# A mixture-of-experts layer on one Trainium2 core: per-row expert weights move from VectorE to GpSimd, and the last normalisation from VectorE to ScalarE, in place

## The reference

```
x   = x + layernorm(attention(layernorm(x)))          # 16 heads of 16, causal
h   = layernorm(x)
scores = softmax(h @ router_weight.T + router_bias)   # 8 experts
topk_w, topk_idx = top_k(scores, 2)
gu  = h @ gate_up_proj[e] + gate_up_bias[e]           # 256 -> 2 x 512
gate = min(gu[:512], 7);  up = clip(gu[512:], -7, 7)
act = (up + 1) * gate * sigmoid(1.702 * gate)
y_e = act @ down_proj[e] + down_bias[e]               # 512 -> 256
x   = x + layernorm(sum over the row's two experts of topk_w * y_e)
```

## Time and profile before

| | |
|---|---|
| median of 3 runs | 2218.0 us (2215.66 to 2218.64) |
| the profiled execution's own time | 2212.91 us |
| its span, first to last instruction | 2211.2 us |
| attention stage | to about 1327 us |
| expert stage | about 1335 to 2143 us |
| combine stage | 2143.6 us to the end |

### The profile page before, as it was taken

One profiled execution on the slowest core, in us unless ns is written; L12 is line 12 of the kernel. 1 busy time (PEld: TensorE's weight loads), 2 busy tenths in 40 slices (PEclk: granted clock), 3 DMA queues, 4 the chain that ended last, 5 costly groups with the idle time before them and its releaser, 6 DMA issues. The chain is left out here.

```text
span 2211.2 us, 51864 instructions
## 1 busy us (share of the span) xinstructions
PE 1984.6 (90%) x13630; PEld 1303.7 (59%) x13631; DVE 1691.3 (76%) x6010; ACT 1131.8 (51%) x2648; POOL 959.5 (43%) x1567
## 2 busy tenths in 40 slices
PE   5899999999999999999989736999999999999950
PEld 4444444444444444444333326999999999999950
DVE  2877788888888888888878245878878788787868
ACT  4377777777777777777767621222222222222210
POOL 5223344455465555564545641333333333333326
PEclk9899999999999999999999958999999999999985
DMA  6525464645464546353553326878788877877866
GB/s 205 174 96 168 147 195 154 193 151 190 127 190 135 180 133 190 124 179 122 184 175 100 120 84 209 243 237 244 236 241 241 234 245 235 243 237 237 244 191 237
DMA packets 259626, 412.93 MB, mean 187 GB/s; under 512 B 37136, under 2 KB 194960, under 8 KB 253200
## 3 DMA queue, kind: packets, MB, share of 16 engines
q1 hardware_dynamic: 219856, 366.67, 51.1%
q0 software_dynamic: 29824, 35.54, 7.6%
q10 hardware_dynamic: 9792, 8.93, 1.5%
HBM read 288.30 MB, written 122.14 MB: 186 GB/s over the span
## 5 line engine op out<-in xcount | busy, mean ns | idle before, releaser
L751 ACT ACTIVATE pw<-ps_e 128x512 f32<-128x512 f32 (+3 forms) x1536 | 687.5, 494 | 282.4 <-PE ps_e L907 268.0
L1300 PE MATMUL ps_g<-x_t,w_gu 128*128 128x128 f32 x4384 | 541.6, 277 | 18.6 <-ACT x_t L1231 11.6
L1300 PEld LDWEIGHTS ps_g<-x_t,w_gu 128*128 128x128 f32 x4384 | 517.8, 192 | 47.3 <-issue 40.7
L520 DVE CUSTOM_DVE_ANT_0 summed<-ps_s,c 128x128 bf16<-128x128 f32 (+3 forms) x1024 | 479.6, 481 | 60.8 <-PE ps_s L888 56.4
L888 PE MATMUL ps_s<-ks,qs 96*128 96x512 bf16 (+3 forms) x1536 | 488.8, 333 | 27.3 <-DVE rmax L520 7.7
L907 PE MATMUL ps_e<-qs,ks 98*128 98x512 bf16 (+3 forms) x1536 | 484.1, 329 | 4.4 <-ACT pw L751 3.5
L523 DVE TENSOR_REDUCE cmax<-ps_s 128x1 f32<-128x512 f32 x512 | 351.3, 686 | 143.4 <-PE ps_s L888 137.7
L888 PEld LDWEIGHTS ps_s<-ks,qs 96*128 96x128 bf16 x1536 | 151.9, 100 | 357.3 <-DVE cmax L520 92.7
L926 PE MATMUL ps_o<-pw,vs 128*32 128x512 f32 (+3 forms) x3072 | 329.1, 501 | 5.1 <-ACT ot L765 2.9
L1252 ACT ACTIVATE d_y<-biased,weight 128x256 f32<-128x256 f32 x136 | 69.1, 508 | 482.0 <-DVE biased L1211 482.0
L435 POOL TENSOR_SCALAR_AFFINE_SELECT pw<-pw 128x512 f32<-128x512 f32 x256 | 163.0, 637 | 302.3 <-ACT pw L751 302.1
(11 more groups left out here) (144 smaller groups left out, 2229.5 us busy)
## 6 DMA issues: line engine op xcount, KB each, us to landing
w_gu<-in_gate_up SPq DMA_DIRECT2D x138, 1024.0 KB
qs<-qk_parts SPq DMA_DIRECT2D x192, 128.0 KB, 2.8
ks<-qk_parts SPq DMA_DIRECT2D x192, 128.0 KB, 2.9
qk_parts<-space SPq DMA_DIRECT2D x120, 192.0 KB
d_xin<-xs SPq DMA_DIRECT2D x139, 130.5 KB
v_aug<-space SPq DMA_DIRECT2D x32, 512.0 KB, 4.6
vs<-v_aug SPq DMA_DIRECT2D x32, 512.0 KB
o_t<-ot SPq DMA_DIRECT2D x64, 256.0 KB
```

What stands on the lines that cost most here:

```text
L520: dve.tensor_tensor_reduce(summed[:, m % RJ, 0:w], ps_s[:, m % RS, 0:w], after[:, HALF - w:HALF], 1.0, LOWEST, ALU.add, ALU.max, dst).then ...
L751: act.activation(pw[:, n % RP, 0:w], ps_e[:, n % RE, 0:w], ACT.Exp, scale=SCALE).then_inc(e_done, 1)
L1300: last = pe.matmul(ps_g[:, u, half, m % KI], w_gu[:, u, k, m * P:(m + 1) * P], x_t[:, u, k], start=(k == 0), stop=(k == KT - 1))
```

## The change

- `destine` leaves DVE and goes to POOL, in five instructions for four: the expert number less the tile's (`other`), is that zero, times the weights, and the sum of the two; and the copy of the place. It runs for tiles 0 to 3 ahead of the first `prepare`, and then `destine(n+3)` stands ahead of `prepare(n)`, that is right behind the add of tile n-1. The waits of PE and ACT on `taken` are as before.
- Padding rows are no longer zero: they come from a new tile `nobody`, which holds the partition number in column 260. The larger-of is gone.
- ACT starts the `x1` load behind the sigmoid of the first tile of a round.
- Combine stage: all 16 steps have buffers of their own and all loads are started at once; the normalisation is four ACT instructions a step (scale and shift), in place; DVE works out the shift; POOL adds in place.

```
@@ clear_ends
-                engine.dma_start(xs[bass.ds(row, P), :], blank[:, 0:ROW]).then_inc(zeros_out, 16)
+                engine.dma_start(xs[bass.ds(row, P), :], nobody[:]).then_inc(zeros_out, 16)
@@ attention stage, gpsimd
+            pool.memset(nobody[:], 0.0).then_inc(blank_set, 1)
+            pool.wait_ge(blank_set, 2)
+            pool.tensor_tensor(nobody[:, D + 4:D + 5], consts["row"], consts["zero"], ALU.add).then_inc(blank_set, 1)
@@ expert stage, vector: destine is gone from hidden and from the start
-                destine(n + 2, i + 1, u)
@@ expert stage, scalar
-                    if pairs.start == 0:
-                        load_x1(act, i)
                     for u in range(2):
                         n = i * 2 + u
                         rows(n + 2, u)
                         sigmoid(n + 1, 1 - u)
+                        if pairs.start == 0 and u == 0:
+                            load_x1(act, i)
@@ expert stage, gpsimd
+            def destine(n, i, u):
+                pool.wait_ge(x_in[u], i * 16 + 16)
+                pool.tensor_tensor(other[:, u], xin[:, u, D + 2:D + 4], expert_f[:, bass.ds(n, 1)].broadcast_to([P, TOPK]), ALU.subtract).then_inc(apart, 1)
+                pool.tensor_copy(place[:, bass.ds(n, 1)], xin[:, u, D + 4:D + 5]).then_inc(taken, 1)
+                pool.wait_ge(apart, n + 1)
+                pool.sem_inc(apart_seen, 1)
+                pool.tensor_scalar(is_it[:, u], other[:, u], 0.0, None, ALU.is_equal).then_inc(is_ready, 1)
+                pool.wait_ge(is_ready, n + 1)
+                pool.tensor_tensor(part_of[:, u], is_it[:, u], xin[:, u, D:D + 2], ALU.mult).then_inc(part_ready, 1)
+                pool.wait_ge(part_ready, n + 1)
+                pool.tensor_tensor(weight[:, bass.ds(n, 1)], part_of[:, u, 0:1], part_of[:, u, 1:2], ALU.add).then_inc(taken, 1)
@@
             with pool.Fori(1, TILES // 2) as i:
                 for u in range(2):
                     n = i * 2 + u
+                    destine(n + 3, i + 1 + u, 1 - u)
                     prepare(n, u)
                     pool.wait_ge(y_out, n * 16)
                     pool.sem_inc(y_free, 1)
                     add(u)
@@ combine stage, scalar
+            def normalise(n):
+                act.wait_ge(shift_ready, n + 1)
+                for c in range(NB):
+                    last = act.activation(moe[:, n, c], moe[:, n, c], ACT.Identity, scale=rstd[:, n, c:c + 1], bias=shift[:, n, c:c + 1])
+                last.then_inc(normed_ready, 1)
@@ combine stage, vector
-                for c in range(NB):
-                    last = dve.tensor_scalar(normed[:, n % 2, c], moe[:, n % RA, c], mv[:, n % 2, c, 0:1],
-                                             rstd[:, n % 2, c:c + 1], ALU.subtract, ALU.mult)
+                dve.scalar_tensor_tensor(shift[:, n], mv[:, n, :, 0], -1.0, rstd[:, n], ALU.mult, ALU.mult).then_inc(shift_ready, 1)
```

More of the change, by code:

```diff
@@ L145, in attention_layer @@
         blank = sb("blank", [P, 1024])
+        nobody = sb("nobody", [P, ROW])
         c16_in = pw[:, 8:10].rearrange("p a b -> p (a b)")[:, 0:const16.shape[1]]
@@ L313, in _ @@
             sp.dma_start(bias_r[:], router_bias.rearrange("(a e) -> a e", a=1).broadcast_to([P, E])).then_inc(c_weights_in, 16)
-            sp.wait_ge(blank_set, 1)
+            sp.wait_ge(blank_set, 3)
             sp.dma_start(acc[0:P], blank[:, 0:D]).then_inc(acc_zero, 16)
             sp.dma_start(xs[DUMMY:DUMMY + SPARE * P].rearrange("(c p) d -> p c d", p=P),
-                         blank[:, 0:ROW].unsqueeze(1).broadcast_to([P, SPARE, ROW])).then_inc(acc_zero, 16)
+                         nobody[:].unsqueeze(1).broadcast_to([P, SPARE, ROW])).then_inc(acc_zero, 16)
             for g in SLOTS:
@@ L1112, in expert_stage @@
         w_gu = sb("w_gu", [P, 2, KT, 2 * I])
+        other = sb("d_other", [P, 2, TOPK])
         is_it = sb("is_it", [P, 2, TOPK])
@@ L1135, in expert_stage @@
                                     "act_ready", "y_ps", "y_biased", "y_ready"))
+        apart, apart_seen = sem("d_apart"), sem("d_apart_seen")
         y_out, one_more = sem("d_y_out"), sem("d_one_more")
@@ L1174, in expert_of, with hidden @@
                 return dve.value_load(table[0:1, 1, bass.ds(n, 1)], min_val=0, max_val=E - 1)
[L1176 to L1187, removed]
+            def hidden(n, u):
                 e = expert_of(n)
@@ L1214, in _ @@
             dve.tensor_scalar(b_gu[:, :, KI:2 * KI], b_gu[:, :, KI:2 * KI], 1.0, None, ALU.add).then_inc(one_more, 1)
-            for u in range(2):
-                destine(u, 0, u)
             dve.wait_ge(one_more, 1)
-            hidden(0, 0, 0)
+            hidden(0, 0)
             with dve.Fori(0, TILES // 2) as i:
-                for n, b, u in ((i * 2 + 1, i, 1), (i * 2 + 2, i + 1, 0)):
-                    hidden(n, b, u)
+                for n, u in ((i * 2 + 1, 1), (i * 2 + 2, 0)):
+                    hidden(n, u)
                     bias_rows(n - 1, 1 - u)
@@ L1270, in _ @@
             pool.sem_inc(carried, 1)
+            for n in range(4):
+                destine(n, n // 2, n % 2)
             prepare(0, 0)
             add(0)
+            destine(4, 2, 0)
             prepare(1, 1)
@@ L1342, in combine_stage @@
     STEPS = 2 * B
-    RA, RO = 6, 3
     with ExitStack() as ctx:
@@ L1349, in sem @@
             return ctx.enter_context(nc.semaphore(name))
[L1351 to L1357, removed]
+        moe = sb("moe", [P, STEPS, NB, D])
+        stats = sb("e_stats", [P, STEPS, NB, 6])
+        mv = sb("e_mv", [P, STEPS, NB, 2])
+        std = sb("e_std", [P, STEPS, NB])
+        rstd = sb("e_rstd", [P, STEPS, NB])
+        shift = sb("e_shift", [P, STEPS, NB])
         pad = sb("e_pad", [P, 1])
[L1359 to L1362, removed]
+        moe_in = [sem(f"e_moe_in{n}") for n in range(STEPS)]
+        out_done = sem("e_out")
+        stats_ready, mv_ready, std_ready, rstd_ready, shift_ready, normed_ready, added = (sem("e_" + n) for n in (
+            "stats_ready", "mv_ready", "std_ready", "rstd_ready", "shift_ready", "normed_ready", "added"))
         acc_v = acc[P:].rearrange("(p s c) d -> s p c d", p=P, s=STEPS)
@@ L1369, in _ @@
         def _(sp):
[L1370 to L1374, removed]
             for n in range(STEPS):
-                if n + RA < STEPS:
-                    sp.wait_ge(normed_ready, n + 1)
-                    load(n + RA)
+                sp.dma_start(moe[:, n], acc_v[n]).then_inc(moe_in[n], 16)
+            for n in range(STEPS):
                 sp.wait_ge(added, n + 1)
-                sp.dma_start(out_v[n], res[:, n % RO]).then_inc(out_done[n % RO], 16)
-            for u in range(RO):
-                sp.wait_ge(out_done[u], len(range(u, STEPS, RO)) * 16)
+                sp.dma_start(out_v[n], moe[:, n]).then_inc(out_done, 16)
+            sp.wait_ge(out_done, STEPS * 16)
         @block.gpsimd
@@ L1389, in _ @@
                 pool.wait_ge(normed_ready, n + 1)
-                if n >= RO:
-                    pool.wait_ge(out_done[n % RO], n // RO * 16)
-                pool.tensor_tensor(res[:, n % RO], normed[:, n % 2], x1[:, n * NB:(n + 1) * NB], ALU.add).then_inc(added, 1)
+                pool.tensor_tensor(moe[:, n], moe[:, n], x1[:, n * NB:(n + 1) * NB], ALU.add).then_inc(added, 1)
         @block.scalar
@@ L1397, in _, with root @@
             act.preload_act_table(ACT.Sqrt)
-            for n in range(STEPS):
+            def root(n):
                 act.wait_ge(mv_ready, n + 1)
-                act.activation(std[:, n % 2], mv[:, n % 2, :, 1], ACT.Sqrt, bias=EPS).then_inc(std_ready, 1)
+                act.activation(std[:, n], mv[:, n, :, 1], ACT.Sqrt, bias=EPS).then_inc(std_ready, 1)
+            def normalise(n):
[3 more added lines that the diff above has]
+                last.then_inc(normed_ready, 1)
+            root(0)
+            for n in range(1, STEPS):
+                root(n)
+                normalise(n - 1)
+            normalise(STEPS - 1)
         @block.vector
@@ L1404, in moments @@
             def moments(n):
-                dve.wait_ge(moe_in[n % RA], (n // RA + 1) * 16)
+                dve.wait_ge(moe_in[n], 16)
                 for c in range(NB):
-                    last = dve.bn_stats(stats[:, n % 2, c], moe[:, n % RA, c])
+                    last = dve.bn_stats(stats[:, n, c], moe[:, n, c])
                 last.then_inc(stats_ready, 1)
@@ L1412, in moments, with scales @@
                 for c in range(NB):
-                    last = dve.bn_aggr(mv[:, n % 2, c], stats[:, n % 2, c])
+                    last = dve.bn_aggr(mv[:, n, c], stats[:, n, c])
                 last.then_inc(mv_ready, 1)
-            def normalise(n):
+            def scales(n):
                 dve.wait_ge(std_ready, n + 1)
-                dve.reciprocal(rstd[:, n % 2], std[:, n % 2]).then_inc(rstd_ready, 1)
+                dve.reciprocal(rstd[:, n], std[:, n]).then_inc(rstd_ready, 1)
```

(11 more changed lines are left out.)

## The result

The changed kernel takes 2279.7 us (median of 4 runs, 2277.7 to 2281.1), the kernel before 2218.3 on the same chip: a ratio of 1.0279, with a 95% interval of 1.0261 to 1.0296. It is 61 us slower. The profiled execution took 2279.2 us, with a span of 2277.4.

The account below looks back on a forecast made before the run. The prediction took DVE to set the loop's pace at 5.78 us a tile. Loop +53.8, start +0.5 and combine stage -16.7 made +37.6 us on the median of 2218.0, say 2255 us, range 2178 to 2297.

Parts of the forecast that it names:

- DVE loses `destine` and stops being the pace: Expert loop: DVE's pace falls from 5.78 to 5.11 us a tile, under PE's floor of 5.52.
- The landing: Expert loop: an add not started early lands about 5.7 us after the weights' issue, when the load's burst is through.
- The locked loop: Expert loop: POOL and PE lock over two tiles, 12.36 us or 6.18 a tile, +53.8 us; chance 0.64.
- six terms: Two-tile loop: landing 5.7, next add 0.8, its issue 1.56, `destine` 1.2, to PE 0.1, to the weights' issue 3.0 us.
- Combine stage: After the loop: without DVE collisions POOL's add of 2.34 us becomes the step, -16.7 us.
- Small edits: Start of the kernel: `nobody` costs nothing, `destine` of the first tiles on POOL +0.5 us.
- fair turns: Rival, loop: add and weight packets interleave, landing 4.5 us or less, 5.58 a tile, total 2167 to 2175; chance 0.18.
- Half way: Rival, loop: landings of 5.0 us or `destine` of 0.7, 5.8 to 5.9 a tile, 2204 to 2218; chance 0.12.
- worse: Rival, loop: PE's idle lowers its clock, or `destine` is 1.8 us; over 6.5 a tile, over 2298; chance 0.06.

Follow-up runs that it names:

- wait_x1_old: The changed kernel with `destine` one tile further ahead, before POOL's wait for the add's landing, and the `x1` load back at the head of ACT's round: 2165.5 us.
- longer: The changed kernel with three more dependent small POOL instructions in `destine`: 2346.0 us, ratio 1.0578 to the kernel before.
- wait_longer: The changed kernel with `destine` one tile further ahead, before POOL's landing wait, plus three more dependent small instructions in it: 2171.1 us, ratio 0.9800.
- one_input: The changed kernel with DVE's two products reading their second input from a PSUM tile of ones instead of SBUF: 2266.1 us, ratio 1.0230.
- combine_only: The kernel before with only the new combine stage: 2200.3 us, ratio 0.9920.
- in_the_wait: The changed kernel with `destine` one tile further ahead, between the preparation of an add and POOL's wait for the landing: 2172.1 us, ratio 0.9795.

## Why the prediction was right

The forecast was 2255, the time is 2280. The mechanism held step by step; two terms of the loop, `destine` and the add's issue, were too small.

- *DVE loses `destine` and stops being the pace.* Right, though before the change it also waited for products in 43 tiles. Now it waits for products in nearly every tile, and once POOL is out of the way (`wait_x1_old`) the loop runs at 5.53, the 5.52 forecast as PE's floor.
- *The landing.* The forecast gave 5.7 us behind the weights' issue. Between 1375 and 2200 us the changed kernel has a median of 5.64 and a mean of 5.61. The 116 adds that start between 0.9 us ahead of the issue and 1.0 behind all land 5.4 to 5.95 behind it, and none of their packets moves before nine tenths of the burst's have; with half a load the mean is 4.37.
- *The locked loop.* Forecast 5.7 + 0.8 + 1.56 + 1.2 + 0.1 + 3.0 = 12.36. In the walk above: 5.57 + 0.75 + 1.62 + 1.41 + 0.06 + 3.06 = 12.47. The adds shown start 0.27 and 0.02 behind the weights' issue, where 0.3 was forecast; over the loop that was no constant: they start from 0.8 ahead to 0.9 behind in turn where tiles alternate, and only half lie within 0.5. The landing stays put all the same, so nothing hung on it. `longer` and `wait_longer` show that the loop spans two tiles and that it is a loop.
- *The mis-sized terms.* The mean tile is 6.37, not 6.18: the loop came to +79.6 us where +53.8 was forecast, and this is all of the miss. The means of the six terms over 130 loops of the changed kernel say where it lies: landing 5.61 (-0.09 against the forecast), next add 0.84 (+0.04), issue 1.69 (+0.13), `destine` 1.43 (+0.23), to PE 0.09 (-0.01), to the weights' issue 3.09 (+0.09): 12.75, 0.39 more in two tiles. `destine` and the add's issue were priced without DVE beside them, and a little low even so. In `one_input`, where nothing stretches them, they are 1.28 and 1.62, and the loop's mean is 12.55. So about half of the miss is the stretching (up to 2.20 for `destine` and 2.12 for an issue); the rest is small: 0.14 of the two terms themselves, 0.07 on the way to the weights' issue. The landing, forecast 0.09 too high, took a little off the miss.
- *Combine stage.* -16.7 forecast, -17.7 in the profile, -17 alone: right, by the row that decides it, POOL's 2.34 us add. ACT's four took 2.08 us.
- *Small edits.* +0.5 forecast ahead of the loop, +4.3 seen, within what `combine_only` shows of the start's own drift.

Of the rivals, *fair turns* falls: landings near the weights' issue are 5.6, not 4.5. The Trainium skill (DMA: Bandwidth & Descriptors, Queues, rings and completion order) has each DMA engine go round its queues a packet at a time; by that rule one would expect a 128 KB add not to wait for a megabyte beside it. The trace doesn't bear this out: 1 packet of the add beside 239 of the weights, and the other 143 behind them. Whether the add's packets were ready to go by then, no run shows, so the cause of their waiting is open. The rival's time, 2167 to 2175, is nonetheless what `in_the_wait` reached, by another way: there PE doesn't wait for the landing at all. *Half way* falls too (6.37, not 5.8 to 5.9). Of *worse*, both halves came true in small part: `destine` reached 1.8 and more in some tiles, and the clock fell behind two of PE's new idle stretches, for 3.4 us of the loop.

## What to carry to other kernels

Before work is moved to an engine with time to spare, look at what it will stand behind in that engine's order: here 1.3 us of work on an engine that idled over 3 us a tile made the loop 80 us longer where it stood behind an instruction that waits for a DMA to land, and 24 to 34 us shorter (5.60 and 5.53 a tile against 5.78) where it stood ahead of that wait. If what waits for the moved work also sets off the transfer that delays it, the two lock; add up the loop once round, divide by the tiles that it spans, and compare with the pace. And where a forecast is taken from quiet rows, ask which instructions of the neighbour engine will lie beside it.

## What the hardware showed

- A POOL instruction of 128 x 2 elements (`is_it`) takes 0.21 us, and 0.57 to 0.67 while DVE runs a product with two inputs in SBUF; the issue of an indirect DMA goes from 1.62 to 2.01 us in the same way. With one of the two inputs in PSUM the longest were 0.23 and 1.68. The Trainium skill (GPSIMD Engine Reference, Specifications) says that POOL shares its SBUF interfaces with VectorE, and collides with instructions that have two SBUF inputs; the traces agree, and add that the issue of an indirect DMA is hit too.
- An accumulating indirect DMA of 128 rows that starts within about half a microsecond of a 1 MB load lands 5.6 us behind that load's issue, and 4.3 to 4.4 behind that of a 512 KB load; its packets move when the load's are through. The fastest of all took 3.7, near the loop's end.
- From the landing to the start of the next add on POOL it takes 0.79 us in the median of the changed kernel's loop, and 0.78 to 0.79 in half of its tiles.
- The granted clock fell to the lower level for some 3.4 us behind each of two stretches of 2.06 us in which PE was idle; a block of 16 matmuls that takes 1.95 us took 2.60 and 2.81. In `one_input` a wait of 2.1 us did not lower it.
